# Two pairs of states' products added by accumulating transfers within SBUF, one norm row from GpSimd to ScalarE, and new order tables

## The reference

```python
def step(h, inp):
    dA_t, dBu_t, C_t = inp
    h = dA_t * h + dBu_t
    y = jnp.einsum('bdn,bn->bd', h, C_t)
    return (h, y)
...
deltaA = jnp.exp(jnp.einsum('bld,dn->bldn', delta, A))
deltaB_u = jnp.einsum('bld,bln,bld->bldn', delta, Bm, x)
...
x = x + _L0_attn_ref(_layernorm(x, axis=-1), ...)
x = x + _L0_ffn_ref(_layernorm(x, axis=-1), ...)
```

## Time and profile before

| | us |
|---|---|
| three runs, median | 2786.84 |
| lowest, highest | 2786.32, 2788.35 |
| profiled execution, its own time | 2788.56 |
| its span, first to last instruction | 2786.8 |
| busy: PE, PE's weight loads | 2721.9, 2476.7 |
| busy: DVE, ACT, POOL | 2707.5, 2721.2, 2705.3 |

### The profile page before, as it was taken

How to read it: one execution, slowest core, us unless ns; L and a number is a source line. 1 busy time by engine, 2 the same in 40 slices (tenths; PEclk the granted TensorE clock), 3 DMA queues, 4 the chain that set the end, 5 groups by cost and what they waited for, 6 DMA issues and landing times.

```text
span 2786.8 us, 58527 instructions
## 1 busy us (share of the span) xinstructions
PE 2721.9 (98%) x22198; PEld 2476.7 (89%) x22260; DVE 2707.5 (97%) x2801; ACT 2721.2 (98%) x4991; POOL 2705.3 (97%) x980
## 2 busy tenths in 40 slices
PE   8999999999999999999999999999999999999988
PEld 6989899889899898998998998989988889989887
DVE  6999999999999999999999999999999999999987
ACT  7999999999999999999999999999999999999994
POOL 4999999999999999999999999999999999999998
PEclk9999999999999999999999999999999999999999
DMA  5345445454454454454554544544545445444442
GB/s 191 96 119 120 122 114 134 119 126 115 107 145 120 118 126 122 112 134 118 126 115 107 145 119 119 124 120 115 134 119 126 115 107 145 119 118 108 118 106 54
DMA packets 261786, 335.30 MB, mean 120 GB/s; under 512 B 157505, under 2 KB 157505, under 8 KB 245122
## 3 DMA queue, kind: packets, MB, share of 16 engines
q1 hardware_dynamic: 228770, 266.55, 32.9%
q0 software_dynamic: 32736, 65.02, 15.4%
HBM read 212.70 MB, written 102.56 MB: 113 GB/s over the span
## 4 chain that ended last, share of the span: by engine, by line
POOL 62%; issue 29%; PE 6%; DVE 1%; DMA 1%; ACT 0%; POOLq 0%; SPq 0%; DVEq 0%; ACTq 0%
POOL A L545 49%; POOL C L562 5%; POOL C L554 2%; POOL out L570 2%; PE Y L797 2%; PE PB L772 2%; POOL XN L497 1%; PE PB L775 1%; POOL PW L514 1%; DVE A L930 1%; PE PM L837 0%; DMA out<-C 0%; PE Y L793 0%; POOL AM L523 0%; POOL SM L489 0%
## 5 line engine op out<-in xcount | busy, mean ns | idle before, releaser
L545 POOL TENSOR_TENSOR A<-A,CB 128x2048 f32<-128x2048 f32 x511 | 2359.7, 4821 | 13.1 <-ACT CAR L616 6.4
L930 DVE TENSOR_TENSOR_SCAN A<-A,CAR,PB 128x512 f32<-128x512 f32 x1536 | 1834.3, 1259 | 24.1 <-PE PB L775 14.4
L609 ACT ACTIVATE A<-DEL,an 128x512 f32<-128x512 f32 x2048 | 1333.7, 715 | 5.9 <-PE Y L797 5.6
L797 PE MATMUL Y<-idf,A 128*128 128x128 f32 x8192 | 1084.5, 273 | 7.9 <-POOL A L545 5.4
L797 PEld LDWEIGHTS Y<-idf,A 128*128 128x128 f32 x8192 | 933.7, 141 | 68.0 <-issue 49.9
L630 ACT ACTIVATE DB<-XN,BC 128x512 f32<-128x512 f32 x1408 | 941.6, 714 | 4.5 <-PE PB L775 4.5
L775 PE MATMUL PB<-idf,DB 128*128 128x128 f32 x5632 | 800.1, 274 | 21.4 <-DVE A L930 13.4
L775 PEld LDWEIGHTS PB<-idf,DB 128*128 128x128 f32 x5632 | 650.3, 141 | 82.0 <-DVE A L930 40.7
L772 PEld LDWEIGHTS PB<-DG,XN 128*128 128x128 f32 x5120 | 606.3, 193 | 34.2 <-issue 31.3
L772 PE MATMUL PB<-DG,XN 128*128 128x128 f32 x5120 | 631.6, 277 | 0.9 <-DVE A L930 0.6
L930 DVE TENSOR_TENSOR_SCAN A<-A,PB 128x512 f32<-128x512 f32 x512 | 585.2, 1201 | 18.2 <-PE PB L775 7.7
(11 more groups left out here) (92 smaller groups left out, 1482.8 us busy)
## 6 DMA issues: line engine op xcount, KB each, us to landing
CB<-c_rows SPq DMA_DIRECT2D x128, 1024.0 KB, 4.9
DG<-b_diag SPq DMA_DIRECT2D x160, 256.0 KB, 5.3
X<-in_x SPq DMA_DIRECT2D x31, 1024.0 KB, 8.0
out<-bib SPq DMA_DIRECT2D x31, 1024.0 KB, 8.9
out<-X POOLq DMA_DIRECT2D x31, 1024.0 KB, 9.5
out<-C POOLq DMA_DIRECT2D x31, 1024.0 KB, 9.2
b_diag<-DG SPq DMA_DIRECT2D x2, 1280.0 KB, 11.8
b_diag<-BC SPq DMA_DIRECT2D x160, 2.0 KB, 3.2
```

The costliest lines, as they stand in the source:

```text
L545: gp.tensor_tensor(A[s % NA][:, :, :], A[s % NA][:, :, :], CB[:, s % (4 * NG), :].unsqueeze(1).broadcast_to([128, KB, L]), ALU.mult).then_ ...
L609: act.activation(A[s % NA][:, g, :], DEL[k % 2][:, g, :], ACT.Exp, scale=an[:, g, n:n + 1])\
L797: i = pe.matmul(Y[j][:, g * 128:(g + 1) * 128], A[s % NA][:, g, j * 128:(j + 1) * 128], idf[:, :], is_transpose=True, start=False, stop=(n ...
L930: dve.tensor_tensor_scan(A[s % NA][:, g, :], A[s % NA][:, g, :], PB[(4 * s + g) % NPB][:, :], init, ALU.mult, ALU.add).then_inc(s_scan, 1)
```

## The change

Each chunk's states 3 and 4, and 9 and 10, become pairs (JOINED = (3, 9)). When POOL has multiplied both by C, it issues a transfer that adds buffer A of the first to buffer A of the second within SBUF, 1 MB read, 1 MB accumulated. PE's `th` leaves states 3 and 9 out and turns the sum with state 4 or 10, behind a wait for the transfer. `decay` of the unit that takes the buffer of state 3 or 9 waits for the transfer in place of `th`. The fourth norm row is done by ACT (NXA = T = 4), and `xn_p` and its semaphore go. All the numbers of PLACES, FIRST and LAST are new, but for idle, last_q, shift0 and a few more; the diff below leaves them out.

```diff
+    JOINED = (3, 9)
     NPB = 3
-    NXP = 1
-    NXA = T - NXP
+    NXA = T
...
+        def turned(s):
+            full, k = divmod(s + 1, NS)
+            return 4 * (full * (NS - len(JOINED)) + len([n for n in range(k) if n not in JOINED]))
+
+        def joined(s):
+            e = len(JOINED) * (s // NS) + JOINED.index(s % NS)
+            return s_jn[e % 2], 16 * (e // 2 + 1)
...
-            def xn_p(p, i):
-                j = NXA + i
-                if i == 0:
-                    gp.wait_ge(s_sh, p + 1)
-                    if p >= 2:
-                        gp.wait_ge(s_tb, 4 * NS * (p - 1))
-                gp.tensor_scalar(XN[p % 2][:, j, :], X[p % NX][:, j, :], SM[:, 2, j:j + 1], SM[:, 3, j:j + 1],
-                                 ALU.mult, ALU.add).then_inc(s_xnp, 1)
...
+            def join(k, d):
+                s = NS * k + JOINED[d]
+                gp.wait_ge(s_mul, s + 2)
+                e = len(JOINED) * k + d
+                if e >= 2:
+                    gp.wait_ge(s_jn[e % 2], 16 * (e // 2))
+                gp.dma_start(A[(s + 1) % NA][:, :, :], A[s % NA][:, :, :], accum_op=ALU.add).then_inc(s_jn[e % 2], 16)
...
                 if g == 0 and s >= NA:
-                    act.wait_ge(s_th, 4 * (s - NA + 1))
+                    if (s - NA) % NS in JOINED:
+                        act.wait_ge(*joined(s - NA))
+                    else:
+                        act.wait_ge(s_th, turned(s - NA))
...
                 s = NS * k + n
+                if n in JOINED:
+                    return
                 if j == 0:
+                    if n - 1 in JOINED:
+                        pe.wait_ge(*joined(s - 1))
...
-                dve.wait_ge(s_th, 4 * NS * (p + 1) - 3 + j)
+                dve.wait_ge(s_th, turned(NS * (p + 1) - 1) - 3 + j)
```

More of the change, by code:

```diff
@@ new lines @@
+        "aggr0": (-1668,),
+        "amax": (1290,),
+        "ascale": (1408,),
+        "b_c": (-448,),
+        "bc_out": (-509,),
+        "bias_p": (20000, 20001, 20002, 20003),
+        "carry": (90, 143, 163, 263, 291, 341, 392, 447, 493, 559, 589, 632, 693, 754, 922, 990),
+        "centre": (1576, 1662, 1663, 1663),
+        "d_t": (-415, -407, -380, -378),
+        "decay": (-181, -146, -129, -128, -63, -14, -13, 68, 75, 77, 111, 124, 145, 160, 168, 176, 207, 219,
+        251, 267, 267, 267, 267, 267, 269, 269, 300, 305, 305, 343, 359, 368, 369, 381, 416, 446, 447, 448,
@@ L30 @@
+        456, 457, 483, 483, 483, 483, 494, 494, 497, 539, 539, 591, 592, 632, 652, 673, 685, 685, 721, 730,
+        735, 735, 735, 752, 758, 764),
+        "delta": (-460, -437, -420, -410),
+        "dl_t": (-235, -168, -108, -103),
+        "du": (-36, -31, -28, -22),
+        "gather": (1202, 1207, 1233, 1265),
         "idle": (2244, 2663, 2696, 3192),
-        "inv": (1332,),
+        "inv": (1294,),
+        "join": (396, 975),
         "last_p": (25000, 25001),
@@ new lines @@
+        "scale_out": (20000, 20001, 20002, 20003),
+        "scale_p": (2081,),
+        "scales": (1295,),
+        "scan": (46, 48, 48, 50, 68, 166, 172, 188, 192, 192, 193, 195, 195, 195, 200, 225, 253, 284, 284,
+        286, 286, 286, 286, 289, 289, 292, 292, 293, 294, 294, 294, 300, 300, 320, 340, 365, 371, 390, 390,
+        396, 396, 398, 398, 398, 400, 502, 647, 675, 675, 881, 881, 881, 881, 881, 909, 909, 918, 920, 968,
+        971, 976, 982, 982, 982),
+        "shift0": (-1049,),
+        "square": (1323, 1323, 1323, 1323),
@@ L69 @@
+        "stats0": (-2560, -2410, -1717, -1683),
+        "step": (1559,),
+        "store_c": (-282,),
+        "store_g": (-19,),
[8 rows of a table added]
+        "times_c": (186, 338, 338, 351, 357, 406, 435, 563, 713, 716, 844, 1023, 1023, 1023, 1023, 1045),
         "turn": (1884,),
[L70 removed]
+        "var1": (1348,),
         "weights": (-475,),
[L72 to L76, removed]
+        "x_p": (-472, -471, -464, -464),
@@ L102 @@
[L102 to L109, removed]
+        "act_b": (-3409, -3409, -3275, -3272, -2320, -1133, -1093, -1092, -1092, -693, -693, -18),
+        "aggr0": (-3211,),
+        "b_c": (-5101,),
+        "bc_out": (-3969,),
+        "carry": (-93, 152),
@@ new lines @@
+        "d_t": (-5101, -5101, -5101, -5101),
+        "decay": (-3422, -3422, -3162, -2483, -1322, -881, -382, -382, -375, -323, 116, 116),
+        "delta": (-3969, -3691, -3603, -3603),
+        "dl_t": (-5101, -5040, -4397, -4394),
+        "du": (-1165, -1165, -1027, -969),
+        "load": (-14880,),
+        "load_c": (-3454, -2763, -1229, 649),
+        "load_g": (-3178, -2786, -2776, -1874, -722),
+        "log0": (-11850,),
+        "rstd0": (-10419,),
+        "scan": (-585, -444, -419, -419, -419, -419, -410, -410),
@@ L110 @@
+        "shift0": (-300,),
+        "stats0": (-9031, -8913, -8913, -8913),
+        "store_c": (-4362,),
+        "store_g": (-4419,),
+        "tb": (-4255, -3818, -2238, -1792, -1737, -1401, -1208, -819),
+        "th": (135, 135, 202, 256),
+        "times_c": (158, 162),
+        "x_p": (-5312, -5232, -5188, -5160),
+        "x_t": (-8713, -5712, -5712, -5626),
+        "xn": (-8816, -8792, -8407, -8265),
+        "xp_out": (-4524,),
         "xt_d": (-1709, -1567),
-        "xt_out": (-5092, -5066, -4701, -4115),
+        "xt_out": (-8265, -6819, -5236, -5200),
@@ new lines @@
+        827, 846, 2347, 2347, 2393, 2472),
+        "add_c": (12193,),
+        "add_x": (5174,),
+        "amax": (5920,),
+        "ascale": (3038,),
+        "centre": (3497, 4344, 4861, 7231),
+        "decay": (-82, -17, -17, -17, 11, 13, 32, 57, 84, 88, 139, 243, 243, 289, 289, 289, 289, 289, 309,
+        322, 331, 365, 366, 440, 471, 477, 477, 484, 484, 484, 558, 570, 570, 578, 579, 596, 596, 596, 629,
+        632, 632, 635, 644, 644, 648, 665, 665, 671, 674, 685, 685, 798, 798, 1050, 1050, 1425, 2451, 4228,
@@ L154 @@
-        "turn": (7911,),
-        "var1": (3546,),
+        "put_bias": (21815,),
+        "q_mm": (33797, 35385, 37377, 38041),
+        "q_t": (17230, 21337, 21701, 28332),
+        "qt_out": (20866, 21564, 21564, 21564),
+        "root": (18046,),
+        "scale_a": (23488, 24759, 24759, 24978),
+        "scale_out": (22856, 23051, 23136, 23514),
+        "scale_p": (10534,),
+        "scales": (6705,),
+        "scan": (-1, 66, 76, 76, 76, 76, 76, 76, 76, 76, 89, 96, 178, 206, 206, 240, 286, 286, 294, 294, 372,
@@ L273, in build @@
         s_th = sem("s_th")
+        s_jn = [sem(f"s_jn{i}") for i in range(2)]
         s_scan = sem("s_scan")
```

133 lines of the change are left out of this document (35 added, 98 removed), and 32 rows, old and new, of tables (LAST, PLACES).

## The result

The changed kernel takes 2839.27 us in the median of 4 runs (2834.25 to 2841.46), against 2786.89 before in the same session: a ratio of 1.0184, with a 95% interval of 1.0171 to 1.0196. It is 52 us slower. The forecast was 2837 with a range of 2804 to 2890.

The account below looks back on a forecast made before the run. POOL and ACT were taken as full at 85.16 us a chunk. POOL's 1.24 + 1.80 - 0.76 - 0.66 = +1.62 gives 86.8, over ACT's 85.70; 31 chunks add 50 us, forecast 2837, range 2804 to 2890.

Parts of the forecast that it names:

- What bounds the kernel: Steady part: POOL and ACT both full, DVE nearly, at 85.16 us a chunk; ACT has 0.17 us a chunk idle.
- step 2: ACT gets the fourth norm row, 0.71 us with 0.17 free, so a chunk can't be shorter than 85.70 us.
- Step 1: PE loses the turning of two of 16 states, 4.2 us a chunk, 136 in all; costed at nothing.
- Step 3: POOL loses the fourth norm row, saving 0.76 us a chunk.
- Step 4: POOL's issue of out<-C, now behind a product, falls from 1.90 to 1.24 us, saving 0.66 a chunk.
- Step 5: POOL issues two more transfers a chunk, costing 1.24 us for the first pair and 1.80 for the second.
- Step 6: Engines waiting for the pairs' transfers: first lands by 16.4 us, needed by 19.0; stalls taken as 0, 2 a chunk for range.
- the second rival: The pairs land late, after 19 us, so PE, DVE, then POOL stand: 2 us a chunk more, 2899 us; chance 0.15.
- Step 7: SP unchanged; DMA's mean share of 0.50 grows by 0.16; CB loads started about two groups ahead, costed at nothing.
- Cheap issues with ACT deciding: POOL pays for issues mostly by the row, so the chunk is 85.7 to 86.0 us, time 2804 to 2812; chance 0.17.
- Not slower: First and last chunk, bound by their own chains, win back at least 17 of 62 us if issues are cheap; chance 0.08.

Follow-up runs that it names:

- no_pairs: The changed kernel without its pairs: PE turns all 16 states, no pair transfer is issued, new orders and ACT's four norm rows stay; 2871.50 us.
- pair_quarter: The changed kernel with each pair's transfer adding only block g = 0, 256 KB in place of 1 MB; 2808.41 us.
- row_on_pool: The changed kernel with the fourth norm row back on POOL and the pairs kept; 2868.28 us.
- before_out_late: The kernel before with one change: POOL issues out<-C behind the next product, not right behind the L562 it waits for; 2786.41 us.
- before_issues: The kernel before, with POOL issuing two more accumulating transfers a chunk, of 128 rows of 4 bytes, that nobody waits for; 2852.75 us.
- late_turn: The changed kernel with PE's turning of states 4 and 5 moved behind state 9's four PB fills; 2881.43 us.
- pair_first: The changed kernel with the first pair's transfer issued ahead of out<-X instead of behind it; 2832.30 us.
- issue_only: The changed kernel with all states turned by PE and, in the pairs' places, accumulating transfers of 128 rows of 4 bytes nobody waits for; 2873.21 us.
- one_pair_9: The changed kernel with only the pair of states 9 and 10; states 3 and 4 are turned apart; 2857.47 us.

## Why the prediction was right, and where it wasn't

The time (2839 for 2837) and the sign were right, and so was the place of the loss, the steady part of a kernel whose ACT and POOL are full. That the size came out so close is luck: two errors cancel. Read from the changed kernel's rows, POOL's own work grew by 1.01 + 1.22 - 0.76 - 0.57 = 0.90 us a chunk, to 86.06, where the prediction had 1.62; and POOL waits 1.0 us a chunk, where it had 0. Together that is the measured 87.08. A third, small one: 1.92 a chunk over the prediction's 31 chunks would be 60 us, but outside the 28 chunks measured the span is 1.3 us shorter.

The runs, taken as a way from one kernel to the other, show how far the parts are from the sum: the norm row costs 16 us, the new orders (out<-C's place among them) 68, PE's relief wins 63 as long as the pairs land early (no_pairs to pair_quarter), and the later landing costs 31.

- **What bounds the kernel, and step 2 (ACT's floor): right**, to 0.02 us a chunk (85.68 for 85.70). 15.6 of the 52 us are the norm row's.
- **Step 1 (PE's relief costed at nothing): wrong for the new orders, untested for the old.** The prediction asked what PE's time was worth beside full engines, and not whether the new order of PE had waits of its own. It has, and without the relief the kernel is 32 us slower (no_pairs). PE's idle time rose from 1.0 to 4.6 us a chunk, by 3.6 where 5 was forecast.
- **Step 3 (the row off POOL): right.** Putting it back costs 0.91 of pitch for the 0.76 (row_on_pool).
- **Step 4 (out<-C): about right in POOL's work, worth little by itself.** In the changed kernel the product ahead of it ends at 1345.53 and the four behind it at 1364.98, so the issue holds POOL for 1364.98 - 4 x 4.53 - 1345.53 = 1.33 us, so 0.57 of the 1.90 are saved, not 0.66. By itself it gave 0.16 of pitch and no time that can be told (before_out_late), since ACT had no more to give.
- **Step 5 (the issues' price): oversized.** The nearest row, 1.355, was for four times as many rows. Measured: 0.91 behind a foreign product and 1.25 behind its own, 2.16 together (before_issues), and 1.01 and 1.22 in the changed kernel, for 3.04. The packet counts in the prediction had named the reason. With the pairs landing early the pitch was 85.98, close to that 86.06 and not 86.8.
- **Step 6 (stalls taken as 0): this failed.** The first pair landed 13.3 us after its issue in the chunk shown, 13.6 after product 4, sooner than the 16.4 that the step allowed; and yet PE stood for it in 20 of 28 chunks. The 19.0 us were worked out from POOL's product 9, but PE reaches that turning earlier, and the fills behind it wait with it. The second pair was given about 4 us to spare, and ACT waited 10.0 us for it. The path through the 7 buffers to ACT was named in the step, and no slack was worked out for it: ACT waited 0.9 us a chunk, over both pairs. The landing costs 1.10 a chunk, 31 us (pair_quarter). So the second rival, with its 2 us a chunk, held half: two of its signs came, PE's wait for the transfer (18.4 us) and DVE's for PE's fills (48.7 for 15.2), and with them a way that it didn't name, the buffers.
- **Step 7 (SP and DMA at nothing): nothing speaks against it.** DMA's share grew from 0.50 to 0.59, the CB loads land in 4.7 us, and no engine's wait is put down to them.
- **The other rivals.** Cheap issues with ACT deciding (2804 to 2812): the issues are cheaper, and with an early landing the time is just there, 2808. Not slower: fell; the first and last chunk gave back 1.3 us.

That ACT's and POOL's waits both end with a shorter landing is shown, but for the smaller load that comes with it. How the 31 us divide between the path over the buffers and that over PE's fills isn't; late_turn and pair_first, in both of which PE's wait for the first pair is all but gone, show that the buffers cost time without it. An eighth buffer A, which would test it alone, wasn't tried, and neither was an earlier second pair. Whether other orders could make the pairs pay stays open too; no run here was faster than before by more than can be told.

## What to carry to other kernels

When several engines are full, an engine's relief is worth at most what the next full one has free, and each addition is paid in full but for what that engine had idle: look for the idle time of each engine in the steady part, and add up. A piece of work handed to a transfer is paid three times over: in its issue on the engine that issues it, in its landing, and in the buffers that it holds meanwhile; work out the slack along each path that waits for the landing, the return of the buffers first. And an order of work is part of a change's price: here the new one cost 68 us without the relief that it came with.

## What the runs showed of the hardware

The issue of a POOL transfer goes by its rows and not by its bytes, as far as three shapes show: 0.93 us for 128 rows, of 4 bytes or of 8 KB alike, and 1.355 for 512 (which also went to HBM).

Two accumulating transfers issued back to back land one after the other: 8.2 and 12.9 us with the pair first, 9.5 and 13.7 with out<-X first. It is not the bytes of the second that take the time: in issue_only the transfer of 128 x 4 bytes, issued 0.8 us behind out<-X, lands in 8.6 to 10.1 us (median 8.8), just when out<-X does (9.5 from its own issue), and those that stand alone in 4.5 (median). (The second pair, with nothing issued just ahead of it, took 10.4 and 10.9 us in the changed kernel and in pair_first and 8.7 in one_pair_9; why it takes more than 8.2 stays open.) The Trainium skill (DMA: Bandwidth & Descriptors, section "Queues, rings and completion order") has each DMA engine take the descriptors of one ring in order, and these landings agree. The same page's fit (section "Anatomy of one DMA") of 2.0 us + bytes / 436e3, an estimate of 4.4 us for 1 MB, doesn't hold for accumulating transfers here: even within SBUF the shortest of 64 took 7.0 us:

```profile
DMA to landing us min/median/max: 7.0/12.0/14.9
```

The tiny transfers of before_issues landed in 3.0 us (median). The chip's clock for PE played no part: the granted clock of the steady stretch was 1.00 in both kernels, although PE's busy share of the span was 94% after and 98% before.
